# Two transformer layers on one core: row swaps of the rotary embedding by chunk, a gelu and a probability copy ahead of a cast on ACT, and a low part later on POOL

## The reference

```python
sin, cos = _rotary_sin_cos(x.shape[1])
q = _apply_rotary(q, sin, cos)   # re = xe*cos - xo*sin ; ro = xo*cos + xe*sin
k = _apply_rotary(k, sin, cos)
scores = jnp.einsum('bhqd,bhkd->bhqk', q, k) / np.sqrt(HD)
...
ff = gelu(h @ ff_w1 + ff_b1) @ ff_w2 + ff_b2     # erf gelu, in both layers
```

## Time and profile before

| | us |
|---|---|
| median of 3 runs | 2088.32 |
| lowest, highest | 2086.74, 2089.87 |
| the profiled execution, its own time | 2085.85 |
| its span, first to last instruction | 2084.0 |
| PE busy | 1845.1 (89%) |
| ACT busy | 1319.0 (63%) |
| DVE busy | 1240.7 (60%) |
| POOL busy | 849.9 (41%) |
| mean granted TensorE clock | 0.971 |

### The profile page before, as it was taken

How to read it: one execution, slowest core, us unless ns; L and a number is a source line. 1 busy time by engine, 2 the same in 40 slices (tenths; PEclk the granted TensorE clock), 3 DMA queues, 4 the chain that set the end, 5 groups by cost and what they waited for, 6 DMA issues and landing times.

```text
span 2084.0 us, 41504 instructions
## 1 busy us (share of the span) xinstructions
PE 1845.1 (89%) x12623; PEld 1664.0 (80%) x12623; DVE 1240.7 (60%) x2973; ACT 1319.0 (63%) x2315; POOL 849.9 (41%) x1036
## 2 busy tenths in 40 slices
PE   4789999999999999997877898888988889888897
PEld 4678888888888888886876888878888788887786
DVE  5566666666666666666653656546655466554651
ACT  3457667776667767775655566666666656656563
POOL 1214333333333333334444445554445544455433
PEclk8899999999999999999998999999999999999999
DMA  6454443333444444343431323223333233332220
GB/s 166 96 128 115 119 121 94 98 98 103 111 117 112 113 121 114 90 103 97 134 92 46 95 83 96 76 75 96 84 92 84 67 96 86 91 86 66 87 62 31
DMA packets 324131, 199.83 MB, mean 96 GB/s; under 512 B 158946, under 2 KB 312548, under 8 KB 324068
## 3 DMA queue, kind: packets, MB, share of 16 engines
q1 hardware_dynamic: 324068, 199.06, 35.7%
HBM read 80.98 MB, written 17.33 MB: 47 GB/s over the span
## 4 chain that ended last, share of the span: by engine, by line
PE 45%; issue 22%; ACT 8%; POOL 6%; DVE 6%; SPq 6%; DMA 5%; POOLq 1%; ACTq 0%; DVEq 0%
PE D L885 10%; PE C L885 9%; PE A L885 7%; PE B L1035 6%; PE B L885 6%; PE B L1021 3%; DMA x_res<-in_x 3%; ACT x_in L682 2%; POOL h_lo L550 2%; SPq L321 2%; ACT hact L739 2%; DMA rotation<-rotation 2%; ACT v_blocks L734 1%; SPq L418 1%; POOL rotation L590 1%
## 5 line engine op out<-in xcount | busy, mean ns | idle before, releaser
L550 POOL TENSOR_TENSOR h_lo<-hact,h_hi 128x512 fp32r<-128x512 f32 x256 | 330.6, 1291 | 341.1 <-ACT h_hi L744 332.6
L885 PE MATMUL D<-wgt_hi,h_hi 128*128 128x256 f32 x1024 | 305.4, 298 | 29.3 <-POOL h_lo L550 22.9
L885 PE MATMUL C<-z_hi,wgt_hi 128*128 128x512 f32 x512 | 218.6, 427 | 106.8 <-ACT hact L739 104.8
L885 PE MATMUL D<-wgt_hi,h_lo 128*128 128x256 f32 x1024 | 291.7, 285 | 0.0
L885 PE MATMUL D<-wgt_lo,h_hi 128*128 128x256 f32 x1024 | 291.2, 284 | 0.0
L885 PE MATMUL A<-k_pad,q_pad 128*128 128x256 f32 x1536 | 259.8, 296 | 12.3 <-DVE exps L1340 5.5
L1035 PEld LDWEIGHTS B<-v_blocks,probs_turned 128*128 128x128 f32 x2048 | 262.2, 201 | 7.1 <-ACT probs_turned L753 2.5
L1035 PE MATMUL B<-v_blocks,probs_turned 128*128 128x68 f32 x2048 | 266.5, 280 | 0.0
L739 ACT ACTIVATE hact<-C,b_col 128x512 f32<-128x512 f32 x256 | 176.4, 689 | 113.7 <-PE C L885 111.3
L1334 DVE TENSOR_REDUCE mx<-A 128x8 f32<-128x512 f32 x256 | 174.3, 681 | 115.7 <-PE A L1007 61.2
L885 PEld LDWEIGHTS D<-wgt_hi,h_hi 128*128 128x128 f32 x1024 | 198.9, 194 | 42.2 <-POOL h_lo L550 20.1
(11 more groups left out here) (138 smaller groups left out, 4258.0 us busy)
## 6 DMA issues: line engine op xcount, KB each, us to landing
k_pad<-k_flat SPq DMA_DIRECT2D x512, 64.0 KB, 2.0
q_pad<-q_flat SPq DMA_DIRECT2D x256, 128.0 KB, 2.3
gates<-gates SPq DMA_DIRECT2D x64, 256.0 KB, 4.3
x_bias<-x_bias SPq DMA_DIRECT2D x32, 512.0 KB, 3.5
rotation<-rotation SPq DMA_DIRECT2D x128, 128.0 KB, 2.1
x_in<-in_x SPq DMA_DIRECT2D x16, 512.0 KB, 3.9
gates<-gated_bias SPq DMA_DIRECT2D x32, 256.0 KB, 4.9
x_res<-in_x SPq DMA_DIRECT2D x16, 512.0 KB, 4.5
```

The lines of the kernel that those rows point to most:

```text
L550: pool.tensor_tensor(hb[1][:, m % 2, :], hact[:, m % 2, :], hb[0][:, m % 2, :].bitcast(F32), ALU.subtract).then_inc(h_lo, 1)
L885: ins = nc.tensor.matmul(dst, l, r, start=first_start and n == 0, stop=last_stop and n == len(todo) - 1, **kw)
```

## The change

Four things change, all in steps in which a is 1, that is, while tile u+1 of layer 1 is being rotated (16 steps).

1. `swap` takes a chunk and not a pair of chunks. It waits for that chunk's sine, and issues four DMAs of 32 partitions by 512 elements where there were four of 32 by 1024 for each pair: 16 DMAs a tile where there were 8. There are four semaphores `swapped0` to `swapped3`. The swap of chunk i waits also until the sum of chunk i-2 has been made, whose place in `rot_swap` it fills.
2. SP issues the swaps of chunks 0, 1 and 2, then the load of the mask row, then the swap of chunk 3.
3. ACT does gelu of part 4 (`hidden(u-1, c, 4)`) and `move_probs(u, 3, 1)` ahead of the cast of chunk 2 (`high_qk(u+1, 1, 2)`).
4. POOL makes the low part of chunk 2 after the sum of chunk 3 and after `hidden_low(u-1, 4)`.

```diff
-        swapped = [sem("keys_swapped"), sem("queries_swapped")]
+        swapped = [sem(f"swapped{i}") for i in range(4)]
...
-            def swap(tile, pair):
-
-                wait_apart(sp, sp_passed, (rot_sined, upto(tile - NT, 4, KC * pair + KC)),
-                           (rot_added, upto(tile - NT, 4, KC * pair)))
+            def swap(tile, i):
+
+                wait_apart(sp, sp_passed, (rot_sined, upto(tile - NT, 4, i + 1)), (rot_added, upto(tile - NT, 4, i - 1)))
                 for e in range(2):
                     for x in range(NX):
-                        sp.dma_start(rot_swap[2 * e + x:P:4, :, :], rot_sin[2 * (1 - e) + x:P:4, :, :])\
-                          .then_inc(swapped[pair], 16)
+                        sp.dma_start(rot_swap[2 * e + x:P:4, i % KC, :], rot_sin[2 * (1 - e) + x:P:4, i % KC, :])\
+                          .then_inc(swapped[i], 16)
...
                 if a == 1:
                     swap(u + 1, 0)
+                    swap(u + 1, 1)
+                    swap(u + 1, 2)
                     wait_apart(sp, sp_passed, (pe_s, upto(u + 1, 2 * G, 0)))
                     sp.dma_start(mrow[:, :].bitcast(F32), mask_tiles[u + 1 - NT].partition_broadcast(P))\
                       .then_inc(mrow_in, 16)
-                    swap(u + 1, 1)
+                    swap(u + 1, 3)
...
             def rotated(tile, i):
-                pool.wait_ge(swapped[i // KC], upto(tile - NT, NSWAP, NSWAP))
+                pool.wait_ge(swapped[i], upto(tile - NT, NSWAP, NSWAP))
...
                     rotated(u + 1, 2)
-                    rotated_low(u + 1, 2)
                 if b is not None:
                     second_rstd(u, 2)
                 if a == 1:
...
                     hidden_low(u - 1, 4)
                 if a == 1:
+                    rotated_low(u + 1, 2)
                     rotated_low(u + 1, 3)
...
                 if a == 0:
                     high_qk(u + 1, 0, 3)
+                if c is not None:
+                    hidden(u - 1, c, 4)
+                if b is not None:
+                    move_probs(u, 3, 1)
                 if a == 1:
                     high_qk(u + 1, 1, 2)
-                if c is not None:
-                    hidden(u - 1, c, 4)
-                if b is not None:
-                    move_probs(u, 3, 1)
...
             def sine(tile, i):
 
                 if i < KC:
-                    await_(dve, swapped[1], upto(tile - NT, NSWAP, 0))
+                    await_(dve, swapped[i + KC], upto(tile - NT, NSWAP, 0))
                 else:
-                    dve.wait_ge(swapped[0], upto(tile - NT, NSWAP, NSWAP))
+                    dve.wait_ge(swapped[i - KC], upto(tile - NT, NSWAP, NSWAP))
```

More of the change, by code:

```diff
@@ L846, in step @@
                     high_qk(u + 1, 0, 3)
-                if a == 1:
-                    high_qk(u + 1, 1, 2)
                 if c is not None:
@@ L852, in step @@
                     move_probs(u, 3, 1)
+                if a == 1:
+                    high_qk(u + 1, 1, 2)
                 if c is not None:
```

## The result

The changed kernel takes 1977.07 us (median, 1976.36 to 1978.04) beside 2089.1 us of the kernel before in the same comparison: a ratio of 0.9463, with an interval of 0.9449 to 0.9477, so 112 us less.

A forecast was written before the change was run, and what follows sets the result against it. PE's waits bound the kernel, chiefly 4.00 us ahead of hidden(5) for a gelu queued behind the swap's DMAs. 16 steps by 5.62 us, 90 us, off 2085.85 gave 1996; 1997 us was said, range 1984 to 2025.

The forecast's parts named there:

- What bounds the kernel: PE's waits bound it, chiefly 4.00 us ahead of hidden(5) for a gelu behind the swap's DMAs, then half clock.
- Small waits: PE's waits of 0.37 us at back(3) and 0.43 us at turn_probs(3,0) both go: hidden(4) 0.80 us earlier.
- Gelu of part 4: On ACT, table load and gelu follow hidden(4) by about 0.1 us; hidden(5) gains 4.54 us, 0.26 us of wait left.
- back(4): PE's back(4) waits for its low part, behind gelu and cast of chunk 2; it gains 4.94 us, POOL's slack 0.4.
- uncovered if ACT were faster: PE's 0.7 us wait at back(5) is covered, ending 0.6 us before hidden(7) could start, unless ACT were faster.
- Clock: PE's clock stays full behind the shorter pauses: 0.68 us less after back(4), so hidden(6) gains 5.62 us.
- hidden(7): At the end of the step hidden(7) still gains 5.62 us; ACT is free in time with 0.3 us slack.
- DMAs: Eight more swap DMAs cost SP 4.8 us a step, hidden; half-sized ones were taken to land in 2.1 us.
- Rivals: Four other outcomes: a new wait, 2024; the clock falling, 2008 to 2023; no effect, 2070 to 2088; slower, 2120 us.
- rival 1: A new wait at back(4), behind cast and sum, takes part of the gain: 2024 us; chance 0.28 shared with falling clock.
- the four short pauses: Rival: PE's clock falls despite only 0.3 to 0.7 us pauses, 2008 to 2023 us; chance 0.28 shared with rival 1.

The follow-up runs named there:

- e1: The kernel before with the swaps by chunk alone, ACT and POOL in their old order: 1978.44 us, ratio 0.9468.
- e2: The kernel before with the new order on ACT alone and the old swaps by pair: 2103.96 us, ratio 1.0069.
- e6: The changed kernel with the swap of chunk 0 released by the sine of chunk 1, as before: 1996.46 us, ratio 0.9553 to the kernel before.
- e5: The changed kernel with ACT's table load for the gelu of part 4 held until PE's hidden(4), in layer 1: 1988.55 us.
- e4: The kernel before with swaps split into 16 half-sized DMAs on four semaphores, still released by pairs: 2084.36 us, ratio 0.9979.
- e3: The kernel before with the new orders on ACT and POOL and the old swaps by pair: 2074.77 us, ratio 0.9934.

## Why the prediction was right or wrong

*What bounds the kernel* was right: the wait ahead of hidden(5), its way back to the swap's DMAs, and the half clock behind it. "So a gelu that depends on nothing rotated waits in line behind a transfer" was half a truth. The gelu did wait in line behind a transfer, but to take it out of the line is worth next to nothing once the swap is early (e1 against the change), and by itself makes the kernel slower (e2), since hidden_low(4) is behind the same transfer by another road. What gives the gain is the start of the swap. The prediction priced the change as a whole and never asked what each part gives alone.

*Small waits* is the first step that failed. 0.80 us was the sum of two brackets; it measured 1.32 (table), and e6 gives back 1.2 when it is undone. A break costs PE more than the idle time in brackets, which the term left at nothing. By 16 steps that is about 8 us of the 20 that were missing.

*Gelu of part 4* is the second. "Table load and gelu follow hidden(4) with a lag of about 0.1 us" was an assumption, taken from the steps of layer 1, where the load came always behind a late cast. The steps of layer 0 in the trace of before had the answer. There the same load stands behind a cast that is on time:

```profile
620.78 1.28 ACT L739 ACT_TABLE_LOAD   x1
623.11 0.69 ACT L739 ACTIVATE hact<-C,b_col 128x512 f32<-128x512 f32 x1 [1.05 <-PE C L885]
```

It began ahead of PE's hidden(4) (621.45) and ended under it, and the gelu then waited 1.05 us for PE. In the changed kernel the load runs ahead in the same way; e5 puts it where the prediction had it, and 11 us come back. With 8 and 11 us added to the sum the forecast would have been 1978.

The Trainium skill (ScalarE: Activation LUTs, What ACT_TABLE_LOAD costs) gives some 1283 ns for a load, and this trace agrees with 1.28 us; it adds a drain of about 1380 ns to every switch, of which no row here shows anything: in before, load and gelu start 1.29 us apart, and the cast ahead had ended 0.02 us before the load.

*back(4)* had the right instruction, the low part, and the wrong thing ahead of it. The path was to run over gelu, cast of chunk 2 and `hidden_high(4)`, with POOL free 0.4 us early. With the gelu 1.9 us earlier than forecast (1287.31 + 32.91 = 1320.22 for 1322.09) that slack became a lack: POOL is busy with the sum of chunk 3 for 0.77 us after `hidden_high(4)` has ended, so the cast that stands between costs nothing, and of the early gelu only a part reaches back(4). The prediction had said what would come, "uncovered if ACT were faster", but of back(5). *Clock* came out near: 0.68 us were forecast between back(4) and hidden(6), and the gain grows there from 6.12 to 6.70. That a pause of 1.25 us brings no half clock was right, but the sum behind it fitted by luck: it set one stretch a step against the mean over the whole run, 0.971, while the mean is 0.86 over the first 130 us, 1.00 from there to 980 us, in layer 0, and 0.97 from 1125 us on. *hidden(7)* was right: nothing is lost or won behind hidden(6).

*DMAs* was right in that eight more of them cost nothing that shows (e4). The Trainium skill's rule to coalesce (DMA: Bandwidth & Descriptors, Rules for kernel authors) speaks of transfers under 64 KB, which the halves just are not, and does not decide here: the trace has 1.9 us for 64 KB and 2.1 for 128 KB, and what the split buys is an earlier start.

*Rivals.* None came in its size. Of rival 1 a small part came: `hidden_low(4)` stands behind the sum of chunk 3, and PE waits 0.23 us for it. The clock did not fall with the four short pauses. Rival 1 named the right place of a new wait (back(4) behind cast and sum), and e2 and e3, where the swap is late, show it at 5.02 and 3.02 us. The range was drawn wide on the side of mishaps and narrow on the other: its lower end took the terms of the sum as if they could only be too large.

## What to carry to other kernels

A wait has to be followed back along each road to what ends last; a reordering that frees one instruction pays only if the others behind the same transfer are freed too, and the cure that worked here was to start the transfer when its own part of the data was there. A bracketed idle time of PE of a few tenths cost nearly twice itself here (0.69 us cost 1.2), so small waits belong in the sum with more than their brackets, in this kernel some 0.25 us more for each. The lower end of a range needs the same care as the upper: ask of each assumed lag what the sum would be without it, and look for the same instruction in another part of the trace, where what stands ahead of it is not late.

## What the runs showed of the hardware

- An ACT_TABLE_LOAD does not always take all waits of the activation behind it: it ran 1.28 us from 1284.07 while the gelu's input came at 1287.3, and held back it costs 0.7 us a step (e5). It is not so for every load: another of the same step of the changed kernel, ahead of the gelu of part 0, itself waited 1.71 us for PE (1259.82). What decides was not tested.
- Behind the same pause of PE the stretch at half clock differed from step to step: in e3, behind 3.0 us, it was some 6.8 us in 9 of the last 14 rotating steps and some 3.4 us in 5; before, behind 4.0 us, 3 and 11 of the 14; in e2, behind 5.0 us, 9 and 5. PE's work at half clock was some 5.0, 3.7 and 4.3 us a step. How long a pause is does not alone tell what it costs; why, stays open. Behind pauses of 1.25 us there was none.
- SP issued the first 12 swap DMAs of a tile over 11.47 us, waits for the sines included. The last four still went out from 1285.24, 0.92 us behind the start of their sine (1284.32), and took 2.38 us to issue; the sum that needs them began 3.79 us after the first of them and is what `hidden_low(4)` stands behind.
